# Where the groups of twelve edge chunks begin, in a three-layer graph convolution on one core

## What is computed

```
def _gcn_conv(x, W, b, src, dst, norm, n_nodes):
    xw = x @ W
    msg = xw[src] * norm[:, None]
    out = jax.ops.segment_sum(msg, dst, num_segments=n_nodes)
    return out + b

src, dst, norm = _gcn_norm(edge_index, n)     # norm = dinv[src] * dinv[dst]
h = _gcn_conv(x, W1, b1, src, dst, norm, n)
h = _gcn_conv(h, W2, b2, src, dst, norm, n)
h = _gcn_conv(h, W3, b3, src, dst, norm, n)
x = _layernorm(x + h, axis=-1)
```

## Time and profile before

| | us |
|---|---|
| median of 3 runs | 2314.16 |
| lowest, highest | 2313.93, 2319.23 |
| profiled execution | 2315.01 |
| its span in the trace | 2313.1 |
| POOL's first and last gather start | 137.5, 2290.6 |
| first gather of layer 1, of layer 2 | 1022.18, 1660.33 |

### The profile page before, as it was taken

How to read it: one execution, slowest core, us unless ns; L and a number is a source line. 1 busy time by engine, 2 the same in 40 slices (tenths; PEclk the granted TensorE clock), 3 DMA queues, 4 the chain that set the end, 5 groups by cost and what they waited for, 6 DMA issues and landing times.

```text
span 2313.1 us, 33066 instructions
## 1 busy us (share of the span) xinstructions
PE 2013.1 (87%) x10242; PEld 1150.3 (50%) x10242; DVE 1491.8 (64%) x3667; ACT 810.3 (35%) x1521; POOL 1621.0 (70%) x1698
## 2 busy tenths in 40 slices
PE   6654778889988887779999999999699999999985
PEld 6321223444444442236666666666366666666642
DVE  8535786777777764445555555556667777777777
ACT  0601554444444433233333333333433333333311
POOL 0257777777777777737777777777577777777774
PEclk7776899999999998999999999999899999999988
DMA  8556888888888887847888888888788888899986
GB/s 285 204 171 180 270 270 241 246 248 248 245 274 265 273 273 236 252 143 233 249 250 250 247 259 275 271 269 283 244 253 269 257 273 273 282 296 297 286 270 217
DMA packets 288154, 585.70 MB, mean 253 GB/s; under 512 B 73203, under 2 KB 132528, under 8 KB 287984
## 3 DMA queue, kind: packets, MB, share of 16 engines
q0 software_dynamic: 132784, 434.04, 61.5%
q1 hardware_dynamic: 155200, 149.59, 19.6%
HBM read 516.40 MB, written 67.06 MB: 252 GB/s over the span
## 4 chain that ended last, share of the span: by engine, by line
POOL 31%; PE 11%; issue 10%; DMA 3%; DVE 1%; DVEq 0%; ACT 0%; POOLq 0%; ACTq 0%
POOL ring L995 31%; PE ps L1322 7%; PE ps L1209 3%; DMA ring<-y_dram,kept 2%; DVE acc L2153 0%; PE ps L1377 0%; PE ps L1220 0%; PE ps L1221 0%; DVE acc L1943 0%; DVEq L1939 0%; DMA y_dram<-acc 0%; PE ps L1372 0%; DVE dense_first L2122 0%; POOLq L308 0%; ACT acc L1475 0%
## 5 line engine op out<-in xcount | busy, mean ns | idle before, releaser
L995 POOL DMA_INDIRECT ring<-y_dram,kept x1650 | 1592.5, 965 | 569.9 <-issue 486.7
L1209 PE MATMUL ps<-ring,onehot 128*32 128x512 f32 x3300 | 463.8, 629 | 111.6 <-DMA ring<-y_dram,kept 110.5
L2153 DVE SCALAR_TENSOR_TENSOR acc<-ps,acc 128x512 f32<-128x512 f32 x494 | 341.3, 691 | 241.2 <-PE ps L1322 210.8
L1322 PE MATMUL ps<-dense_first,wide_a 128*128 128x512 f32 x1144 | 318.0, 399 | 14.6 <-DVE dense_first L2122 6.5
L1565 ACT CAST wide_a<-onehot 128x512 fp32r<-128x512 uint8 (+1 forms) x297 | 173.5, 594 | 266.9 <-PE ps L1322 188.3
L1322 PEld LDWEIGHTS ps<-dense_first,wide_a 128*128 128x128 f32 x1144 | 211.4, 189 | 104.8 <-issue 28.6
L1943 DVE SCALAR_TENSOR_TENSOR acc<-ps,mask,acc 128x512 f32 x280 | 197.3, 746 | 70.9 <-issue 68.6
L1322 PE MATMUL ps<-dense_next,wide_a 128*128 128x512 f32 x820 | 237.5, 398 | 1.2 <-DVE acc L2153 1.2
L1908 DVE TENSOR_TENSOR onehot<-ps,kept 128x128 f32<-128x128 f32 x417 | 119.4, 287 | 157.6 <-PE ps L1209 155.9
L1322 PE MATMUL ps<-dense_first,y_rows 128*128 128x512 f32 x756 | 210.5, 400 | 2.5 <-DVE dense_next L2122 1.6
L1209 PEld LDWEIGHTS ps<-ring,onehot 128*32 128x32 f32 x3300 | 69.9, 109 | 274.6 <-issue 270.5
(11 more groups left out here) (286 smaller groups left out, 2298.5 us busy)
## 6 DMA issues: line engine op xcount, KB each, us to landing
onehot<-a_dram SPq DMA_DIRECT2D x456, 64.0 KB
ring<-y_dram,kept POOLq DMA_INDIRECT x1650, 4.7
y_dram<-acc SPq DMA_DIRECT2D x99, 256.0 KB, 11.3
a_dram<-ring SPq DMA_DIRECT2D x19, 784.0 KB, 5.6
acc<-in_x_dram SPq DMA_DIRECT2D x1, 12288.0 KB
y_dram<-acc SPq DMA_DIRECT2D x12, 1024.0 KB, 12.1
out_dram<-acc SPq DMA_DIRECT2D x48, 256.0 KB
w_sb<-in_x_dram SPq DMA_DIRECT2D x24, 256.0 KB
```

The lines of the kernel that those rows point to most:

```text
L995: pool.indirect_dma_start(ring[:, s, :], None, y_dram[layer], bass.IndirectOffsetOnAxis(ap=rows, axis=0)).then_inc(done, 16)
L1209: mm = pe.matmul(ps[k * WIDE:(k + 1) * WIDE, g % BANKS, :], wide_hot[:, r, k, :], ring[:, r * CPQ + k, :], start=opens, stop=closes, tile_ ...
L1322: mm = pe.matmul(ps[:, bank, :], wide_slots[n % WIDE_SLOTS][:, P * k:P * (k + 1)], y_parts[(TILES * (layer - 1) + tile) % YSLOTS][:, part, :],
L2153: dve.scalar_tensor_tensor(out=rows, in0=ps[:, UNIT_BANKS[n % len(UNIT_BANKS)], :], scalar=0.5, in1=rows, op0=ALU.mult, op1=ALU.add).then_ ...
```

## The change

Groups begin at chunk 10 + 12k. The sparse part of layer 0 then begins at chunk 118 (was 120), that of layers 1 and 2 at chunk 298 (was 288), so that the edges of ten more chunks are counted into `a_dram`. Group 64 is the last, with chunks 778 to 781: a quad of two and two quads of one. `SPARE`, which bounds how far the edge list may run late, falls from 15 to 8 chunks, so that tiles are known to be complete earlier; only tile 48 now ends with the last group, and `FINISH` holds 48 tiles. `last_tiles` becomes `last_tile` on PE, ACT, DVE and SP, without the loop over two tiles. In `add_group` the load of the tile number stands ahead of the wait for the placing. Quads: 168, 123 and 123. Gathers: 664, 484 and 484. The units spread over the quads by the same formulas: in layers 1 and 2 two quads fewer hold them, in layer 0 `UNITS0_TO` is 134 and not 137.

```
+OFFSET = 10
-SPARE = 15 * P
+SPARE = 8 * P
...
-    GROUPS = -(-USED // CPG)
-    CHUNKS = GROUPS * CPG
+    GROUPS = -(-(USED - OFFSET) // CPG)
+    CHUNKS = OFFSET + GROUPS * CPG
...
-        return (P * (EDGES // N) * tiles - DENSE_SPARE) // (P * CPG)
+        return ((P * (EDGES // N) * tiles - DENSE_SPARE) // P - OFFSET) // CPG
+    def group_chunk(own):
+        return OFFSET + own * CPG
...
-        return [c for c in range(own * CPG + a, (own + 1) * CPG, CPW) if c < USED]
+        return [c for c in range(group_chunk(own) + a, group_chunk(own + 1), CPW) if c < USED]
...
-    UNITS0_TO = LAYER_QUADS[0] - 6 - 3 * EARLY_DENSE
+    UNITS0_TO = LAYER_QUADS[0] - 10 - 3 * EARLY_DENSE
-    LOOP_TILES = TILES - 2
+    LOOP_TILES = TILES - 1
...
-                pe.wait_ge(h_ready, LOOP_TILES)
-                for j in range(2):
-                    rows = tile_of(LOOP_TILES + j)
-                    for k in range(FB):
-                        mm = pe.transpose(ps[:, LAST_TURN_BANKS[j], k * P:(k + 1) * P], rows[:, k * P:(k + 1) * P], ident[:, :])
-                    mm.then_inc(tile_turned, 1)
+                for k in range(FB):
+                    mm = pe.transpose(ps[:, LAST_TURN_BANK, k * P:(k + 1) * P], tile_of(TILES - 1)[:, k * P:(k + 1) * P], ident[:, :])
+                mm.then_inc(tile_turned, 1)
...
             def add_group(g, units=0, residuals=0):
+                own = own_of(g)
+                t = dve.value_load(group_tile[0:1, own:own + 1], min_val=0, max_val=TILES - 1)
                 dve.wait_ge(placed, g + 1)
                 if g + 2 < ALL_GROUPS:
                     stage_group(g + 2)
...
-                own = own_of(g)
-                t = dve.value_load(group_tile[0:1, own:own + 1], min_val=0, max_val=TILES - 1)
                 for part in range(2):
```

More of the change, by code:

```diff
@@ L171, in gcn_three_layers_resnorm @@
     BLOCK_OF = [b for b in range(BLOCKS) for _ in block_of(b)]
-    LAST_GROUP = [min(GROUPS - 1, (P * (EDGES // N) * (t + 1) + SPARE - 1) // (P * CPG)) for t in range(TILES)]
+    LAST_GROUP = [min(GROUPS - 1, group_with((P * (EDGES // N) * (t + 1) + SPARE - 1) // P)) for t in range(TILES)]
     def source0(k):
@@ L378, in gcn_three_layers_resnorm @@
         turned_sb = w2_sb[:, 1, :]
-        last_turned = [w2_sb[:, 2 + k, :] for k in range(2)]
-        last_h = [h_sb, row_sb]
+        last_turned = w2_sb[:, 2, :]
+        last_h = row_sb
         any_onehot = onehot[:, 0:QUADS, :, :].rearrange("p q c n -> p (q c) n")
@@ L916, in dense_layer, with last_tile @@
                         store_rows(layer, t)
[L918 to L926, removed]
+            def last_tile(layer):
+                t = TILES - 1
+                if layer < LAYERS - 1:
+                    store(layer, t)
+                else:
+                    sp.wait_ge(o_ready, t + 1)
+                    for a, rows in parts_of(t):
+                        sp.dma_start(node_rows(out, t, a, rows), tile_of(t)[a:a + rows, :]).then_inc(o_stored, 16)
             with order_holds(sp):
@@ L942, in _ @@
                         start_dense(layer + 1)
-                    last_tiles(layer)
+                    last_tile(layer)
                     if layer == 0:
@@ L1360, in first_layer, with last_tile @@
                         dense0_unit(u)
-            def last_tiles(layer):
+            def last_tile(layer):
                 place_group(GROUP_AT[layer + 1] - 1)
@@ L2219, in first_layer, with last_tile @@
                         low0(k)
-            def last_tiles(layer):
+            def last_tile(layer):
                 add_group(GROUP_AT[layer + 1] - 1, units_before(layer, BLOCKS) if layer > 0 else 0)
                 dve.wait_ge(added, 2 * GROUP_AT[layer + 1])
-                for k in range(2):
-                    t = LOOP_TILES + k
-                    if layer < LAYERS - 1:
-                        bias_rows(layer, t, last_h[k], LAST_PRODUCT_BANK + k)
-                    else:
-                        begin_norm(t, t)
-                if layer == LAYERS - 1:
-                    for k in range(2):
-                        finish_norm(LOOP_TILES + k, LOOP_TILES + k)
+                if layer < LAYERS - 1:
+                    bias_rows(layer, TILES - 1, last_h, LAST_PRODUCT_BANK)
+                else:
+                    begin_norm(TILES - 1, TILES - 1)
+                    finish_norm(TILES - 1, TILES - 1)
             def stage_any(i):
```

63 lines of the change are left out of this document (32 added, 31 removed).

## The result

The changed kernel takes **2288.76 us** (median of four runs: 2282.94, 2288.19, 2289.33, 2289.90); the kernel before took 2314.05 beside it. The ratio is 0.9882, 95% interval 0.9859 to 0.9906: faster by 25.3 us by the medians, by 27 us (22 to 33) by the ratio. The forecast was 2286, with 2280 to 2297 around it.

The account below looks back on a forecast made before the run. The prediction took POOL's gathers to bound the kernel, with PE close behind. Its terms -25.0, -1.7, -1.9 and -0.1 summed to -28.7 us, giving a forecast of 2286 us, range 2280 to 2297.

Parts of the forecast that it names:

- Gathers, -25.0: Layers 1 and 2: ten gathers fewer each, at a pitch of 1.25 us, save 25.0 us if POOL keeps the pace.
- Layer 0's added gathers, 0: Last group of layer 0: two added gathers land well before they are needed and cost 0 (2.5 us without that cover).
- The middle, 0: Middles of layers 1 and 2: PE's waits and the ring absorb the denser work, POOL is not held, cost 0.
- The end of layer 0, -1.7: End of layer 0: edits pulling against each other sum to -1.7 us, bounds -3.5 and +2.5.
- (a): End of layer 0: the last tile but one becomes the loop's last and its transposes need group 63's adds, +2.1 us.
- (b): End of layer 0: the end phase multiplies one tile, 8 matmuls and not 16, -3.6 to -2.3 us, summed as -3.0.
- (c): End of layer 0: the tile-number load ahead of the wait saves 0.4 us for each of two groups.
- The end of layer 1, -1.9: End of layer 1: a split's queue, a tile-number load and a second bias row fall away, -1.9 us, bounds -2.5 and 0.
- The end of layer 2, -0.1: End of layer 2: VectorE's norms and adds change the end by -0.1 us beyond the gathers, bounds -1.5 and +3.
- PE in layer 2: Rival: PE sets the pace in layer 2, which keeps 7.4 of its 12.5 us; 2293 to 2294 us, chance 0.14.
- in both: Rival: PE sets the pace in layers 1 and 2, in all 14.8 us less; 2301 us, chance 0.06.
- Layer 0 kept its pace: Judges the rival that denser layer 0 leaves POOL's pace, at +0.25 us a quad 42 us, 2327 us; chance 0.03.

Follow-up runs that it names:

- ten-gather kernel: The kernel before with ten gathers left out in each of layers 1 and 2, all else in place: 2286.77 us for 2315.42, ratio 0.9877.
- the one with thirty fewer and a relieved PE: The kernel before, thirty gathers fewer in each of layers 1 and 2, their dense units multiplying only the rows' high part: 2240.74 us, ratio 0.9673.
- shallow ring: The changed kernel, but POOL waits for the sum three quads back rather than five: 2300.08 us, ratio 0.9927 to the kernel before.
- the dose of thirty: The kernel before with thirty gathers left out in each of layers 1 and 2: 2282.48 us, ratio 0.9855.
- the load of the tile number: The changed kernel with that load behind the waits again, on two slow chips: 2670.26 us beside 2661.76, and 2699.59 beside 2680.83 for the changed kernel.

## Why the prediction was right, and where its steps were not

**What bounds the kernel: right.** The shares of busy time point to PE, and POOL's waits to POOL. The ten-gather kernel and the one with thirty fewer and a relieved PE decide it: 28.7 / 20 = 1.43 (1.2 to 1.6) and 74.7 / 60 = 1.245 us saved for each gather gone, with no gather held.

**Gathers, -25.0: right within the measurement, with one thing missed.** The pitch of 1.25 us holds. But in the profiled pair layers 1 and 2 became 15.7 us shorter each, not 12.5, and the other 3.2 are fewer long gathers. I had assumed that the time above the median gather stays. Summed over the gathers of layer 2 it went from 14.1 us to 10.8, but four executions with the old grid have 14.1, 10.7, 11.5 and 11.4 there and two with the new one 10.8 and 12.0, so this is scatter. In layer 1 the two grids don't overlap: the four with the old one (before, ten fewer, and the two with thirty fewer) have 5.2, 4.6, 4.6 and 5.1 us over the median, the two with the new one (after, shallow ring) 2.0 and 2.5. By these means the term for layer 1 was too small by some 2.7. The section on the hardware says where this comes from.

**Layer 0's added gathers, 0: right in kind.** They landed before they were needed: the adds of the last group start at 1007.69, some 14 us after the last landing (989.06, and 4.4 us from issue to landing at the median). But the forecast's sign for it, a gap before layer 1 of 28.7 us, was not seen: the gap is 31.45.

**The middle, 0: right.** PE's waits went to 4.3 and 2.5 us (said: some 4, and next to nothing), the lag of the sum to 9.9 us at quad 104 of layer 2 (said: at most 13.3), POOL was never held. The reserve was real but is nearly spent: the dose of thirty shows what comes next.

**The end of layer 0, -1.7: wrong, and the step that failed is the clock.** The timeline of PE (start, duration, operation, idle before it) at the end of layer 0:

```profile
983.39 1.93 PE L1216 MATMUL ps<-ring,onehot 128*32 128x512 f32 x8 [4.29 <-DMA ring<-y_dram,kept]
...
988.48 1.94 PE L1216 MATMUL ps<-ring,onehot 128*32 128x512 f32 x8 [2.11 <-DMA ring<-y_dram,kept]
990.35 5.65 PE L1258 MATMUL ps<-w,w_sb 128*128 128x512 f32 x8
...
999.95 0.66 PE L1242 MATMUL ps<-ident,acc 128*128 128x128 f32 x4 [0.79 <-DVE acc L1945]
1000.53 1.05 PE L1216 MATMUL ps<-ring,onehot 128*32 128x512 f32 x2
1001.51 3.70 PE L1258 MATMUL ps<-w,w_sb 128*128 128x512 f32 x8
...
1011.01 5.55 PE L1380 MATMUL ps<-w,w_sb 128*128 128x512 f32 x8 [0.75 <-ACT w_sb L1624]
```

and the windows around it, first of after, then of the same place before (us, busy us by engine, granted clock, DMA share, GB/s):

```profile
984.00:988.40 4.40, 2.37 (x12) 0.72 (x4) 0.29 (x1) 0.60 (x1) 3.18 (x5) 0.50 0.88 305
988.40:1001.50 13.10, 11.73 (x30) 3.60 (x30) 3.70 (x8) 1.90 (x3) 0.66 (x1) 0.77 0.22 70
```

```profile
986.00:990.50 4.50, 1.65 (x12) 0.60 (x12) 0.29 (x1) 0.85 (x2) 2.69 (x3) 1.00 0.96 342
```

The prediction looked for the half clock only in the very last products; here it comes earlier. PE waits 4.29 us for a gather, and the sum at 983.39 and all up to 994 us run at half the clock. In the 12 us that end with the 660th gather PE is busy for 61% with the new grid (after, and shallow ring alike), for 72 to 88% in the four executions with the old end. The likely reason is that the tiles that finish in the loop do so earlier now (8 spare chunks, not 15, and dense units that end some quads from where they did); no run changed that alone on an undisturbed chip. The sum behind the 660th gather takes 1.94 us for 1.06 and the product 5.65 for 3.70, 2.8 us that no step of mine had. The kernel with the shallow ring shows the same drop at this place (a sum of 1.93 us). Of the four executions with the old end only the one with the relieved PE does, and it is the one that needs 37.1 us below. The rest is near what I said: (a) from the 660th gather's end to the start of the loop's last product it is 17.44 us for 11.99; without the 2.8 of the clock that is +2.6, of which 0.6 is a later start of the sum, so +2.0 for +2.1; (b) eight matmuls take 5.55 us (6.76 with the shallow ring) for 9.29, -3.7 for -3.0; (c) the first add starts 0.27 us after the staging for 0.81, so -0.54 at each of two places for -0.4. From the 660th gather's end to layer 1's first gather it is 36.4 us, and 36.9 with the shallow ring; the old end has 35.4, 33.6, 34.5 and 37.1. By the means the end of layer 0 became some 1.5 us longer and not 1.7 shorter; with 3.5 us between equal ends, one execution of each couldn't have told.

**The end of layer 1, -1.9: right.** The gap before layer 2 is 15.5 us, and 14.6 with the shallow ring, for 15.9, 16.9 and 17.3 in the three old ones whose PE had no lag: -1.6 on average. In the profiled pair alone it was -0.4.

**The end of layer 2, -0.1: not settled.** From the last gather's end it is 22.95 and 18.8 us with the new grid, 21.5, 21.2 and 22.1 with the old. In the profile of after PE idles before the last full sum and is at half clock behind it (the sum takes 1.94 us), and VectorE splits the last group only when three norms are through:

```profile
2258.44 1.94 PE L1216 MATMUL ps<-ring,onehot 128*32 128x512 f32 x8 [3.73 <-DMA ring<-y_dram,kept]
...
2272.25 0.68 DVE L1927 TENSOR_TENSOR place_rows<-ps,place_rows 64x512 fp32r<-64x512 f32 x1
...
2277.45 0.55 DVE L2025 TENSOR_SCALAR acc<-acc,ln 128x512 f32<-128x512 f32 x1
```

**The sum.** -28.7 was forecast, -25.3 measured by the medians, -27 by the ratio. The gathers alone, put at -25.0, gave -28.7 in the experiment (-25 to -32), and the ends near nothing instead of -3.7; in the traces the clock at the end of layer 0 is the largest part of that. So two terms missed in opposite ways, and that the total lies so near is partly luck; that the experiment shows just the -28.7 of the forecast's sum is chance.

**The rivals.** PE in layer 2 (0.14) and in both (0.06) didn't come, but the thirty-gather kernel shows that rival at a dose three times as high. Layer 0 kept its pace: the 660th gather ended at 984.07 for 986.80, the difference being long gathers.

## What to carry to other kernels

Read the bound from the waits of the engine that issues, not from busy shares alone: here an engine 98.7% busy in the middle stayed the follower, because its waits and the ring's depth left room for what the change took from the other. Count that room in both currencies (its waits, and how far it may lag before the ring holds the leader) and remember that a lag comes back at the next barrier (here 12 of 43.6 us). And when work is moved away from just before a barrier, look at what PE's clock does there: behind a wait of 4.29 us, a sum and a product took 2.8 us longer.

## What the runs showed of the hardware

**Long gathers are a matter of phase.** In layer 1 every gather over 1 us (20 before, 7 after) runs beside a low-part split of VectorE, a subtraction with both operands and its result in SBUF. The pair from the profile of before, VectorE first:

```profile
1345.65 0.68 DVE L2122 TENSOR_TENSOR dense_next<-w,dense_next 128x512 fp32r<-128x512 f32 x1
...
1345.70 1.45 POOL L995 DMA_INDIRECT ring<-y_dram,kept  x1 [0.30 <-issue]
```

And a pair from the profile of after, the other way round:

```profile
1343.11 0.95 POOL L1002 DMA_INDIRECT ring<-y_dram,kept  x1 [0.30 <-issue]
...
1343.81 0.68 DVE L2124 TENSOR_TENSOR dense_next<-bias,dense_next 128x512 fp32r<-128x512 f32 x1
```

**The same program ran 16 to 18% longer on two other chips**, in all of its runs. The instructions' own times are nearly the same: a gather's median is 946 to 949 ns, a unit's matmul 389 ns at the median on both, by the mean 410 for 398, as the clock was at half more often (0.90 over the span for 0.94). What grows is the time from an instruction's end to the start of the one that waits for it. The changed kernel in layer 1 there, PE's unit and VectorE's add of it:

```profile
1308.31 0.61 PE L1329 MATMUL ps<-dense_first,wide_a 128*128 128x512 f32 x2
...
1312.00 0.69 DVE L2155 SCALAR_TENSOR_TENSOR acc<-ps,acc 128x512 f32<-128x512 f32 x1 [3.57 <-remote]
```

The unit has ended by 1308.92 and VectorE is idle, but its add starts 3.1 us later. Between 1300 and 1500 us an add that found VectorE idle started 0.04 us after its unit's last matmul, at the median and at most, on the undisturbed chips (54 adds in the profile of after). In the profiles of the changed kernel on the slow ones VectorE stood idle for 2.0 and 1.9 us at the median between the two, 4.9 and 5.2 at the ninth decile, and up to 6.3. The add also waits for a signal of VectorE's own, so it isn't settled which signal is late, nor what delays it. An experiment that compares within one such chip (the load of the tile number, 8.5 to 19 us) measures another bound than the one in question.
